# Heads and sums moved within SBUF, stack loads spread over units, a W2 product ahead of feed_out

## What is computed

```python
xn1 = _ln(x, g1, be1)
sa = _mha(xn1, xn1, Wq_s, bq_s, Wk_s, bk_s, Wv_s, bv_s, causal=True)
x = x + (sa @ W1 + b1)
xn2 = _ln(x, g2, be2)
ca = _mha(xn2, encoder_out, Wq_c, bq_c, Wk_c, bk_c, Wv_c, bv_c, causal=False)
x = x + (ca @ W2 + b2)
xn3 = _ln(x, g3, be3)
ff = jax.nn.relu(xn3 @ Wf1 + bf1) @ Wf2 + bf2
return x + ff
```

## Time and profile before

| | |
|---|---|
| median of 3 runs | 621.04 us (619.91 to 627.74) |
| profiled execution: its time | 619.56 us |
| its span | 617.8 us |
| mean granted clock of TensorE | 0.892 of full |
| busy: PE, DVE, ACT, POOL | 503.6, 347.1, 305.9, 181.8 us |
| DMA moved | 56.51 MB |

### The profile page before, as it was taken

The page is one execution under the profiler, slowest core; times in us unless marked ns, Lnnn a source line. Parts: engine busy times, 40 slices in busy tenths (PEclk is TensorE's granted clock), DMA queues, the critical chain, the costliest instruction groups (busy, mean ns, idle before and its releaser), DMA issues.

```text
span 617.8 us, 8792 instructions
## 1 busy us (share of the span) xinstructions
PE 503.6 (82%) x3296; PEld 293.8 (48%) x3296; DVE 347.1 (56%) x669; ACT 305.9 (50%) x590; POOL 181.8 (29%) x276
## 2 busy tenths in 40 slices
PE   1769876999997999899987667569586667989887
PEld 1656642444443444344432254324223347988877
DVE  4756985888786887778420247525231753454431
ACT  3444213686775675667576403437251535253460
POOL 3875940221221213121325313223040450121200
PEclk9979985999999999899999877758555968999999
DMA  8253963062829073709510385887333112101001
GB/s 290 76 163 124 184 153 70 2 88 53 131 76 142 2 137 95 118 7 83 164 63 16 112 173 108 138 112 147 98 110 106 69 42 68 35 1 35 18 18 35
DMA packets 42890, 56.51 MB, mean 91 GB/s; under 512 B 13024, under 2 KB 29152, under 8 KB 42848
## 3 DMA queue, kind: packets, MB, share of 16 engines
q1 hardware_dynamic: 40544, 47.56, 37.9%
q10 hardware_dynamic: 2304, 8.39, 4.0%
HBM read 35.12 MB, written 20.42 MB: 90 GB/s over the span
## 4 chain that ended last, share of the span: by engine, by line
PE 55%; DMA 17%; DVE 13%; ACT 5%; SPq 4%; issue 3%; POOL 3%; ACTq 0%; DVEq 0%
PE ps L882 12%; PE ps L971 11%; PE ps L996 11%; PE ps L934 10%; DMA stacks<-shift_t 6%; PE ps L1083 5%; DMA arena_h<-heads 4%; DMA recips<-recip_rows 4%; DVE max_a L1162 4%; DVE xn L1117 3%; ACT arena_p L755 3%; PE ps L956 2%; PE ps L866 2%; PE ps L938 2%; SPq L412 2%
## 5 line engine op out<-in xcount | busy, mean ns | idle before, releaser
L755 ACT ACTIVATE arena_p<-ps 128x512 f32<-128x512 f32 (+4 forms) x416 | 190.3, 542 | 129.6 <-PE ps L971 127.5
L1162 DVE TENSOR_REDUCE max_a<-ps 128x1 f32<-128x512 f32 (+4 forms) x280 | 159.4, 619 | 47.3 <-PE ps L934 35.8
L971 PE MATMUL ps<-stacks 99*128 99x512 bf16 (+2 forms) x448 | 149.5, 367 | 28.4 <-DMA stacks<-shift_t 23.3
L934 PE MATMUL ps<-stacks 96*128 96x77 bf16 (+4 forms) x640 | 143.3, 300 | 19.3 <-DVE max_a L1162 16.2
L934 PEld LDWEIGHTS ps<-stacks 96*128 96x128 bf16 x640 | 58.0, 110 | 83.8 <-DVE max_a L1162 42.6
L996 PE MATMUL ps<-arena_p,v_group 128*32 128x512 f32 (+4 forms) x896 | 94.1, 540 | 0.7 <-POOL arena_p L629 0.5
L629 POOL TENSOR_SCALAR_AFFINE_SELECT arena_p<-arena_p 128x512 f32<-128x512 f32 x64 | 40.9, 651 | 167.7 <-ACT arena_p L755 167.7
L971 PEld LDWEIGHTS ps<-stacks 99*128 99x128 bf16 (+1 forms) x448 | 45.3, 107 | 93.4 <-ACT arena_p L755 37.3
L1162 DVE TENSOR_REDUCE max_b<-ps 128x1 f32<-128x384 f32 (+3 forms) x88 | 52.5, 635 | 20.6 <-PE ps L938 20.6
L882 PE MATMUL ps<-wf2r,hid_r 128*128 128x256 f32 x384 | 48.6, 289 | 8.7 <-DVE hid_r L1277 8.7
L882 PEld LDWEIGHTS ps<-wf2r,hid_r 128*128 128x128 f32 x384 | 47.8, 197 | 9.8 <-DVE hid_r L1277 9.8
(11 more groups left out here) (67 smaller groups left out, 501.7 us busy)
## 6 DMA issues: line engine op xcount, KB each, us to landing
heads<-out_t ACTq DMA_DIRECT2D x16, 512.0 KB, 4.5
stacks<-qc_parts SPq DMA_DIRECT2D x48, 128.0 KB, 5.0
stacks<-q_parts SPq DMA_DIRECT2D x42, 128.0 KB, 5.0
stacks<-k_parts SPq DMA_DIRECT2D x42, 128.0 KB, 7.5
arena_h<-heads SPq DMA_DIRECT2D x8, 512.0 KB
recips<-recip_rows SPq DMA_DIRECT2D x8, 512.0 KB
q_parts<-parts SPq DMA_DIRECT2D x8, 384.0 KB, 2.6
k_parts<-parts SPq DMA_DIRECT2D x8, 384.0 KB, 2.8
```

Source lines behind the costliest of these rows:

```text
L755: nc.scalar.activation(probs[0:a.kp, a.probs_slot(g, ui), h, k * BANK:k * BANK + width], ps[0:a.kp, unit % S_BANKS, 0:width], ACT.Exp, sca ...
L934: ins = nc.tensor.matmul(m_bank(use)[:, o:o + w], q_stack[0:ROWS, g % a.nb, h, t * P:(t + 1) * P], k_rows(ROWS, g, h, s0, s0 + w), start=T ...
L971: ins = nc.tensor.matmul(ps[0:keys, unit % S_BANKS, lo - k * BANK:hi - k * BANK], k_rows(ROWS_S, g, h, i * P, i * P + keys), q_stack[:, g ...
L1162: nc.vector.tensor_reduce(dst, m_bank(use)[:, 0:nh * w].rearrange("p (h w) -> p h w", h=nh), AX.X, ALU.max).then_inc(s.max_read, 1)
```

## The change

Three edits.

1. `heads_dram`, `store_out` and `load_heads` go. `pack_sums` moves the 4 rows of sums and `pack_heads` the 4 x 16 head rows (four DMAs of 64 KB) from `out_t` straight to `sums` and `heads_out`. SP issues them at unit 8 of the next group in SELF and at unit 4 in CROSS, once ACT's copy is done; for the last group ACT issues the sums. `copy_out` now waits until both kinds of the group before have landed. `moves` changes: inverses are taken, stored and spread earlier, in SELF all at the last unit of step 1 (unit 15), in CROSS at units 0, 1 and 2 two groups later instead of 0, 1 and 3 three groups later.
2. `load_stacks` is issued block by block: in SELF that of g+2 at units 0, 2, ... 22 of g, in CROSS that of g+4 at units 0 to 5 of g. The wait in front of each block is the same, for the scores of the buffer's last user.
3. In the feed-forward the W2 product stands ahead of `feed_out(n)`, and DVE's order follows.

```diff
-            ends = [max(u for u, (ui, _, _) in enumerate(self.units) if ui == step) for step in (2, 3, 3, 3, 5)]
-            self.moves = dict(zip(("loaded", "inverted", "stored", "spread", "divided"), ((1, u) for u in ends)))
+            ends = [max(u for u, (ui, _, _) in enumerate(self.units) if ui == step) for step in (1, 1, 1, 3)]
+            self.moves = dict(zip(("inverted", "stored", "spread", "divided"), ((1, u) for u in ends)))
-            self.moves = {"loaded": (2, 4), "inverted": (3, 0), "stored": (3, 1), "spread": (3, 3), "divided": (3, 6)}
+            self.moves = {"inverted": (2, 0), "stored": (2, 1), "spread": (2, 2), "divided": (2, 7)}
+        self.packed = 2 * GH if causal else GH
+        self.load_at = [2 * b for b in range(2 * len(QP))] if causal else list(range(len(QP)))
...
+        def pack_sums(eng, s, g):
+            eng.wait_ge(s.out_copied, g + 1)
+            at_least(eng, s.recips_stored, 16 * (g // 2))
+            r0 = GW * (g % 2)
+            eng.dma_start(sums[r0:r0 + GW, :],
+                          out_t[D::2 * D, :].rearrange("h (s c) -> h s c", c=sums.shape[1])).then_inc(s.sums_in, 16)
+        def pack_heads(eng, s, g):
+            eng.wait_ge(s.out_copied, g + 1)
+            r0 = GW * (g % 2)
+            for h in range(GH):
+                eng.dma_start(heads_out[r0 + h * D:r0 + (h + 1) * D, g // 2, :],
+                              out_t[2 * D * h:2 * D * h + D, :]).then_inc(s.heads_in, 16)
...
                 for op, *what in a.pe[lo:hi]:
-                    if op == "score" and a.behind("loaded", *what) is not None:
-                        load_heads(a.behind("loaded", *what))
+                    if op == "score" and what[1] == a.packed and what[0]:
+                        pack_sums(sp, s, what[0] - 1)
+                        pack_heads(sp, s, what[0] - 1)
                     if op == "score" and a.behind("stored", *what) is not None:
                         store_recips(a.behind("stored", *what))
                     if op == "score" and a.behind("spread", *what) is not None:
                         spread_recips(a.behind("spread", *what))
...
-                    if op == "score" and what[1] + 1 == len(a.units):
-                        if what[0] + a.nb < NG:
-                            load_stacks(a, s, what[0] + a.nb)
+                    if op == "score" and what[0] and what[1] in a.load_at:
+                        blk = a.load_at.index(what[1])
+                        if what[0] - 1 + a.nb < NG:
+                            load_stacks(a, s, what[0] - 1 + a.nb, [blk])
...
                 def copy_out(g):
                     act.wait_ge(s.pv, a.n_steps * (g + 1))
-                    at_least(act, s.heads_stored, 16 * g)
+                    at_least(act, s.sums_in, 16 * g)
+                    at_least(act, s.heads_in, 16 * GH * g)
...
-                feed_out(n)
                 if n + 2 < NCH:
                     heads_product(2 * NCH + n + 2, S2, W2)
+                feed_out(n)
```

More of the change, by code:

```diff
@@ L408, in store_parts, with load_blocks @@
                     sp.dma_start(dst, parts[:, u % 4, :, c0:c0 + w]).then_inc(parts_out[u % 4], 16)
-            def load_blocks(src, dst, which, gs, arrived, lo=0, hi=None):
-                for blk in range(len(QP)):
+            def load_blocks(src, dst, which, gs, arrived, lo=0, hi=None, blks=range(len(QP))):
+                for blk in blks:
                     sp.dma_start(dst[blk * D:(blk + 1) * D, :, lo:hi],
@@ L423, in load_half, with load_stacks @@
                 load_blocks(k_dram, k_self[:, 0, :, :], KP, slice(0, 1), arrived, lo, hi)
-            def load_stacks(a, s, g):
+            def load_stacks(a, s, g, blks=range(2 * len(QP))):
                 par = g % a.nb
                 at_least(sp, s.scores, len(a.units) * (g - a.nb + 1))
-                load_blocks(q_dram if a.causal else qc_dram, q_stack[:, par, :, :], QP, slice(g, g + 1), s.q_in[par])
+                q_blks = [b for b in blks if b < len(QP)]
+                load_blocks(q_dram if a.causal else qc_dram, q_stack[:, par, :, :], QP, slice(g, g + 1), s.q_in[par],
+                            blks=q_blks)
                 if a.causal:
-                    load_blocks(k_dram, k_self[:, par, :, :], KP, slice(g, g + 1), s.q_in[par])
+                    load_blocks(k_dram, k_self[:, par, :, :], KP, slice(g, g + 1), s.q_in[par],
+                                blks=[b - len(QP) for b in blks if b >= len(QP)])
             def attention(a, s, lo, hi=None):
@@ L441, in load_shift @@
                             .then_inc(s.shift_in[g % a.nb], 16)
[L443 to L452, removed]
                 def store_recips(g):
@@ L485, in attention @@
                         sp.dma_start(wf2, w_f2.rearrange("(k p) n -> p k n", p=P)).then_inc(ff_in, 16)
-                    if op == "score" and what[1] + 1 == len(a.units):
-                        if what[0] + a.nb < NG:
-                            load_stacks(a, s, what[0] + a.nb)
-                        if a.causal and what[0] == NG - 3:
+                    if op == "score" and what[0] and what[1] in a.load_at:
+                        blk = a.load_at.index(what[1])
+                        if what[0] - 1 + a.nb < NG:
+                            load_stacks(a, s, what[0] - 1 + a.nb, [blk])
+                        if a.causal and what[0] == NG - 2 and blk < len(KP):
                             sp.wait_ge(S1.scores, len(a.units) * (NG - 2))
-                            load_blocks(kc_dram, k_ctx.rearrange("p g h t -> p (g h) t"), KP, slice(0, NG), S2.k_in)
+                            load_blocks(kc_dram, k_ctx.rearrange("p g h t -> p (g h) t"), KP, slice(0, NG), S2.k_in,
+                                        blks=[blk])
                 if hi is None:
+                    pack_heads(sp, s, NG - 1)
                     for g in range(NG):
-                        if g in a.left("loaded"):
-                            load_heads(g)
                         if g in a.left("stored"):
@@ L772, in attention @@
                         exp(*what)
-                        if copied is not None:
-                            store_out(copied)
-                            copied = None
                     if op == "score" and a.step_end(*what) == 0 and what[0]:
-                        copied = what[0] - 1
-                        copy_out(copied)
-                if copied is not None:
-                    store_out(copied)
+                        copy_out(what[0] - 1)
                 if not a.causal:
@@ L783, in attention @@
                 copy_out(NG - 1)
-                store_out(NG - 1)
+                pack_sums(act, s, NG - 1)
             act.wait_ge(wqkv_in, 16)
@@ L1196, in divide_heads @@
                     dve.wait_ge(s.recips_in, 16 * (g // 2 + 1))
+                    dve.wait_ge(s.heads_in, 16 * GH * (g + 1))
                     o = heads_out[:, g // 2, :]
@@ L1249, in _ @@
             dve.wait_ge(S1.pv, SELF.n_steps * NG)
-            split(U_QC)
             invert_sums(NG - 1)
-            for u in range(1, 4):
+            for u in range(4):
                 split(U_QC + u)
@@ L1278, in hidden_low_halves @@
                                             ALU.subtract).then_inc(hid_low, 1)
-            if NG - 3 in CROSS.left("inverted"):
-                invert_sums(NG - 3)
             xn_low_half(0)
@@ L1284, in _ @@
                 if n == 0:
-                    hidden_low_halves(n, range(0, 1))
-                    divide_heads(NG - 3)
-                    hidden_low_halves(n, range(1, 4))
+                    hidden_low_halves(n, range(0, 2))
                     invert_sums(NG - 1)
+                    hidden_low_halves(n, range(2, 4))
                     hidden_low_halves(n, range(4, FF // P))
@@ L1302, in _ @@
                     xn_low_half(n + 1)
+                if n + 2 < NCH:
+                    add_rows(("w", 2 * NCH + n + 2), n + 2, NCH + n + 2)
+                    ln_sums(2 * NCH + n + 2)
                 add_rows(("f", n), n, 2 * NCH + n)
```

15 lines of the change are left out of this document (3 added, 12 removed).

## The result

The changed kernel took 643.97 us (median of 4 runs, 639.63 to 650.2) against 620.47 us before (median of 4; the prediction counts from 621.04, the median of 3): ratio 1.0401, 95% interval 1.0333 to 1.0469. The ratios here compare fast runs alone: a run over 1.5% above the fastest of the same kernel, such as that of 650.2 us, is left out of them as slow. The changed kernel is 4% slower; 614.6 was predicted, in a range of 600 to 627. The profiled execution took 642.71 us with a span of 641.0.

The account below looks back on a forecast made before the run. PE was taken to bound SELF and the feed-forward, DMA waits the rest. SELF +8.7, between the attentions -7.6, CROSS -6.0 and feed-forward -1.5 sum to -6.4 us: 621.04 - 6.4 = 614.6 us, range 600 to 627.

Parts of the forecast that it names:

- What bounds the kernel: PE in SELF, stopped at two group changes; a DMA chain without PE between the attentions; DVE's DMA waits in CROSS.
- SELF, what goes: In SELF both stops for shift rows (5.9 us) and the low clock after the second (1.6) vanish: gain 7.5 us.
- SELF, what comes: In SELF late blocks cost 12.2 us in groups 2 and 4, 1.0 in odd groups, and low clock 3.0.
- The bound of 7.6: Upper bound on SELF's block lateness in groups 2 and 4, if packs cost more and the store queues longer: 7.6 us.
- The odd groups: In SELF's odd groups blocks 4 to 11 count at T+12.7, 0.3 us late, three times: 1.0 us.
- Between the stages: Between SELF and CROSS the sums skip store and reload through DRAM, so the spread lands at 349.7 instead of 357.23: -7.6 us.
- CROSS: In the second attention 1 us gained at 1.2 GHz, 2 and 2.5 by faster clock, 0.5 by one inverse less: -6.0 us.
- a better clock: In CROSS fewer, shorter stops let part run at 2.4 GHz, 2 us, and the rows products run fast, 2.5 us.
- Feed-forward: Chunk 0 gains 0.5 us plus 0.4 in feed_out, chunk 1 gains 0.6 as the product fills a wait: -1.5 us.
- SP as the bound: Rival, chance 0.12: SP stands at `pack_sums` while blocks, shift and inverses queue behind; slower by 11.6 us, 632.6 us.
- point of decision: In SELF, blocks 8 to 11 landing later than T+17, where its stops cost more than the gains there and between stages.

Follow-up runs that it names:

- e6: The changed kernel with SELF's blocks at units 0 to 11, SELF's divide at unit 43 and CROSS's stack loads in one go: 604.01 us, ratio 0.976.
- e5: The changed kernel with each row of inverses stored twice and the spread read from 16 rows instead of 8: 636.82 us, ratio 1.0294.
- e1: The changed kernel with SELF's blocks at units 0 to 11 instead of 0, 2, ... 22: 618.85 us, ratio 0.9991.
- e2: The changed kernel with edit 2 alone undone, stack loads in one go in SELF and CROSS: 613.82 us, ratio 0.9886.
- e8: The changed kernel with CROSS's stack loads in one go behind unit 7 as before, SELF as changed: 638.82 us, ratio 1.0336.
- e11: e6 with edit 3 undone, the W2 product behind feed_out again: 601.76 us, ratio 0.9756.
- e7: The changed kernel with SELF's spread moved from unit 15 to 23 and its divide to unit 43: 624.21 us, ratio 1.0112.

## Why the prediction was wrong

The forecast was -6.4 us and the profiles differ by +23.2. Of the 29.6 us between them 18.5 stand in one term, what comes in SELF, and 9.9 in CROSS.

**What bounds the kernel** was right: PE in SELF, stopped by DMA at group changes, DMA alone between the stages.

**SELF, what goes** (-7.5) was right. e6 has nothing but these removals left in SELF and its last copy comes 8.8 us earlier than before, 1.0 of them already there in group 0, which leaves 7.8.

**SELF, what comes** (+16.2) is the step that failed, by its sizes: the text named the stops, their place, their groups and their order, and in the end they cost 34.7 us (what the five intervals exceed 28.0 by), against 16.2. Term by term, with T the end of the last product as in the prediction:

| in groups 2 and 4 | predicted | group 2 | group 4 |
|---|---|---|---|
| block 4 issued | T+3.2 | T+5.5 | T+4.3 |
| store issued | T+5.7 | T+7.5 | T+6.3 |
| store landed, spread issued | T+8.5 | T+11.4 | T+10.9 |
| first chunk of g+2 | T+18.5 | T+23.9 | T+23.4 |
| PE due there | T+12.4 | T+12.6 | T+12.5 |

Three errors add up. The packs were priced at 0.37 us per issue from ACT's one large store and cost 0.6 to 0.9 (2.44 to 3.60 for four), so the store was issued 1.8 and 0.6 us late. The store of 32 KB took 3.9 us (group 2) and 4.6 (group 4) behind four blocks, where 2.8 was allowed. And from the spread's issue to PE's start I allowed 10.0 us and it took 12.5: half the engines first finished the spread and then their share of four blocks, which e5 bears out. The 10.0 also holds a slip: T+8.5 + 7.24 less 1 is T+14.7, and the text went on from T+14.2. The bound of 7.6 was itself too low; I had widened each term a little instead of putting all at their dear end. The odd groups, 0.3 us each by the prediction, took 1.42, 1.82 and 1.83; in group 3 block 4 was issued at T+4.3 too, 1.1 us later than priced. What the intervals hold beyond the 27.3 us of stops, 7.4 us, is mainly the low clock: 3.9 in groups 2 and 4, where 3.0 was forecast, and 3.2 in group 5, where none was.

**The divide in SELF** has no term in the prediction, so DVE's wait for the spread at unit 31 was put at nothing without a reason. In the changed kernel PE's stops hid it; e1 showed that without them the spread lands behind unit 31, a stop of 3.34 and 2.12 us.

**Between the stages** (-7.6; the text's own times give 7.5) measured -6.0, the mechanism as forecast. The sums landed 3.7 us after the start of ACT's copy (363.94 to 367.60), as forecast. But the divide stood behind the fourth split, 0.7 us later than the forecast landing of the spread, and took 2.13 us where it took 1.23 before: these are the missing 1.6.

**CROSS** (-6.0) measured +3.9, and here 4.5 of the 6.0 us were a better clock, 2 for the stage and 2.5 for the rows product. It did not come: the granted clock fell from 0.68 to 0.65, five of the six products up to the rows product took 3.64 us (four of six before), and the rows product at 496.95 took 3.62 us for 8 matmuls, the slow value, where it took 3.75 before. The late blocks held PE for 5.47 and 2.28 us instead of 2.3 once, but PE's idle time in the stretch rose by 0.7 us only. e2 and e8, with the loads in one go, took 139.0 and 142.2 us. The stage is not steady, though: e6 and e11 have the same code there and took 142.0 us at a clock of 0.69 and 137.8 at 0.74, so single profiles settle nothing below some 4 us, and what late blocks and divides each cost in CROSS stays open.

**Feed-forward** (-1.5) measured -1.2, by the two steps forecast: the divide held the product 2.81 us, DVE's order held feed_out(1) 1.13 us. e11, without edit 3, has 114.7 us there, less than the 116.5 of the changed kernel and the 117.7 before: the gain is that of edit 1, whose inverse comes early, and no run shows one for the order.

**The rivals.** "SP as the bound", with 0.12, named what happened, at half its price. Its point of decision, blocks landing behind T+17, was the right one to look at, though by the forecast's own terms it lies at T+18: there two stops of 5.6 us with 1.0 and 3.0 make up the 7.5 and 7.6 of gains. The forecast had put T+18.5 into its own sum, past that point, and still came out as a gain of 6.4 us, because CROSS was credited with 6.0, of which 4.5 were a better clock that no row supported.

## What to carry to other kernels

An instruction stream that only waits on semaphores is not paced by the unit at which a DMA is written; what paces it is the first wait that does not hold yet, so list one in-order queue with all its users and ask for each what it will stand behind. Put bulk loads ahead of anything that waits for a round trip, and put the consumer of a round trip a full period behind it: the three moves of order in e6 turned a loss of 4.0% into a gain of 2.4% (ratio 1.0401 to 0.976), where leaving out edit 2 gave 1.1% (e2). When a transfer read from 8 rows keeps half of the DMA engines (share about one half from 182 to 186 in group 2) and the next one needs all of them, the second is as late as the first on that half; reading it from 16 rows took 4.0 and 4.6 us off the long stops (e5).

## What was unexpected of the hardware

A plain issue of a DMA by SP took 0.6 us (0.9 in group 2) for 16 rows of 4 KB within SBUF, more than the 0.33 us of ACT's issue of 128 such rows. The store of 32 KB landed 1.49 us after its issue alone and 3.9 and 4.6 us behind four blocks.

A stop of 1.83 us in group 5 was followed by the 1.2 GHz level (window below, granted clock third from the end), and that interval took 33.0 us; the stop of 1.82 in group 3 had no such sequel, and its interval took 30.0. Nor does the length order them in other runs: e7's stop of 2.09 us was followed by a clock of 1.00, and e5's of 1.70 in group 5 by 0.58 within 2 us. So the price of a stop of some 2 us was 0.2 us beyond itself in one case and 3 in another.

```profile
292.00:296.00 4.00, 4.00 (x26) 1.47 (x23) 1.81 (x3) 0.99 (x3) 0.64 (x1) 0.50 0.00 0
```
